# A Mamba selective scan laid out as 4 states x 32 channels on the partitions, with column-strip sums

## What is computed

```
for t in range(L):                      # per batch b, channel d, state n
    h[d, n] = exp(dt[d, t] * A[d, n]) * h[d, n] + dt[d, t] * x[d, t] * Bm[n, t]
    y[d, t] = sum over n of h[d, n] * Cm[n, t]
y = (y + D[d] * x[d, t]) * silu(z)
```

## Time and profile before

| | |
|---|---|
| median of 3 runs | 3600.76 us (3592.4 to 3601.16) |
| the profiled execution | 3599.16 us |
| its span in the profile | 3597.9 us |
| mean granted TensorE clock | 0.966 of full speed |
| busy share over the span | PE 90%, PEld 66%, DVE 61%, ACT 42%, POOL 39% |
| transfers | 273.15 MB, mean 76 GB/s |

### The profile page before, as it was taken

How to read it: one execution, slowest core, us unless ns; L and a number is a source line. 1 busy time by engine, 2 the same in 40 slices (tenths; PEclk the granted TensorE clock), 3 DMA queues, 4 the chain that set the end, 5 groups by cost and what they waited for, 6 DMA issues and landing times. The chain is left out here.

```text
span 3597.9 us, 41339 instructions
## 1 busy us (share of the span) xinstructions
PE 3225.9 (90%) x12763; PEld 2392.0 (66%) x12763; DVE 2197.2 (61%) x1925; ACT 1514.3 (42%) x2148; POOL 1395.1 (39%) x794
## 2 busy tenths in 40 slices
PE   9999677877876689999799999997889999999996
PEld 7877433333332277888577777776668888888884
DVE  6544499999999955711376777774553333333326
ACT  4447644444444332311387778773231121121111
POOL 0002299999999722000377777770100000000001
PEclk9999889999999999999899999998999999999998
DMA  2124521113110075322111111115211111111101
GB/s 110 41 83 160 201 109 61 45 52 143 45 61 30 18 275 198 131 87 93 64 34 34 31 31 35 31 31 195 82 65 47 41 54 47 41 55 52 47 18 58
DMA packets 125427, 273.15 MB, mean 76 GB/s; under 512 B 24448, under 2 KB 38656, under 8 KB 122400
## 3 DMA queue, kind: packets, MB, share of 16 engines
q1 hardware_dynamic: 107632, 262.42, 21.3%
q10 hardware_dynamic: 17712, 9.79, 0.9%
HBM read 207.87 MB, written 64.29 MB: 76 GB/s over the span
## 5 line engine op out<-in xcount | busy, mean ns | idle before, releaser
L799 PE MATMUL scan_ps_y<-scan_g,scan_ident 128*128 128x512 f32 x1024 | 514.3, 635 | 192.1 <-DVE scan_g L730 175.0
L771 POOL TENSOR_TENSOR scan_dbx<-scan_u,scan_b_bc 128x1024 f32<-128x1024 f32 x256 | 594.2, 2354 | 31.9 <-DMA scan_b_bc<-bc 31.9
L1549 POOL TENSOR_TENSOR at_p_lo<-at_p,at_p_hi 128x512 fp32r<-128x512 f32 x384 | 513.3, 1344 | 175.9 <-ACT at_p_hi L1457 163.7
L702 ACT ACTIVATE scan_ps_a<-scan_dt,scan_a_neg 128x512 f32<-128x512 f32 x512 | 328.0, 679 | 442.9 <-DVE scan_g L730 435.8
L799 PEld LDWEIGHTS scan_ps_y<-scan_g,scan_ident 128*128 128x128 f32 x1024 | 191.8, 198 | 481.9 <-DVE scan_g L730 297.5
L927 POOL TENSOR_TENSOR ff_y<-ff_y,ff_rstd 128x512 f32<-128x512 f32 x14 | 24.9, 1806 | 1126.7 <-DVE ff_rstd L916 1126.7
L743 DVE TENSOR_TENSOR_SCAN scan_ps_a<-scan_ps_a,scan_dbx 128x512 f32<-128x512 f32 x384 | 441.6, 1211 | 1.5 <-POOL scan_dbx L771 1.5
L1495 DVE TENSOR_REDUCE at_neg_max<-at_ps_mx 128x1 fp32r<-128x1536 f32 x132 | 231.9, 1757 | 173.6 <-PE at_ps_mx L1569 162.4
L1454 ACT ACTIVATE at_p<-at_ps_s 128x512 f32<-128x512 f32 x384 | 228.1, 594 | 117.5 <-PE at_ps_s L1586 96.3
L1969 DVE TENSOR_TENSOR ff_hf<-ff_sg,ff_ps_u 128x1024 f32<-128x1024 f32 x28 | 34.2, 1221 | 388.6 <-PE ff_ps_u L97 388.6
L1457 ACT ACTIVATE at_p_hi<-at_p 128x512 fp32r<-128x512 f32 x384 | 242.8, 632 | 12.3
(11 more groups left out here) (253 smaller groups left out, 7215.0 us busy)
## 6 DMA issues: line engine op xcount, KB each, us to landing
ff_w<-in_w SPq DMA_DIRECT2D x56, 512.0 KB, 4.2
in_w<-in_w_in SPq DMA_DIRECT2D x32, 512.0 KB, 3.6
mid_w<-in_w_out SPq DMA_DIRECT2D x32, 512.0 KB, 5.3
ff_w<-in_w SPq DMA_DIRECT2D x56, 256.0 KB, 2.6
ff_wo_wo<-in_w_o SPq DMA_DIRECT2D x32, 384.0 KB, 3.1
scan_cx<-in_ctx SPq DMA_DIRECT2D x9, 1024.0 KB, 5.7
sz<-in_xz SPq DMA_DIRECT2D x16, 512.0 KB, 3.1
dt<-in_acc SPq DMA_DIRECT2D x16, 512.0 KB, 3.6
```

Of the source, the lines that this page charges most:

```text
L702: nc.scalar.activation(ps_a[(2 * s + k) % SB][:, h], dt[s][:], ACT.Exp, scale=a_neg[:, it, 2 * k + h:2 * k + h + 1]).then_inc(a_ready, 1)
L771: nc.gpsimd.tensor_tensor(dbx[k % SL][:], u[s][:].unsqueeze(1).to_broadcast([P, 2, L]), b_bc[:, 2 * k:2 * k + 2], ALU.mult).then_inc(dbx_r ...
L799: last = nc.tensor.matmul(ps_y[:], ident[:], g[(2 * s + k) % SB][:, h], start=False, stop=k == NK - 1 and h == 1)
L1549: nc.gpsimd.tensor_tensor(p_lo[t % NSL][:], p[t % NSL][:], f32(p_hi[t % NSL][:]), ALU.subtract).then_inc(p_lo_done, 1)
```

## The change

A block is still 128 channels of one batch, but the partitions now hold 4 groups of states x 32 channels: partition 32a + d is channel d of a strip, and its states are the four of group a. The 128 channels are CG = 4 strips c of CW = 32, which lie along the free dimension. So:

- dt and u are loaded four times, once for each group of partitions, as [128, 4, 512] (`load_spread`: 4 transfers of 256 KB for each tile, where there was one). Two slots each, where there were three.
- The rows of Bm and Cm are loaded with 4 rows to each group of 32 partitions (`load_rows`), for both batches before the loop; nothing is loaded at the change of batch.
- A pair k is now two strips (c = 2(k % 2) and the next) of the state k // 2 of each group. It is still 1024 elements on 128 partitions, and there are still 8 pairs a block.
- DVE scans the pair in one instruction of 1024 elements. A zero decay at element 512, written once before the loop (ACT's second exponential writes elements 513 to 1023), makes the second strip start anew.
- All scans write `g` in SBUF, and all products with Cm are made in place in `g`; 4 slots of `g`, 2 of `ps_a`. A decay slot is free after its scan, where it was free after the product for six pairs of eight.
- PE sums with a [128, 32] selector `sel` (4 identities stacked): each 512 elements are added into a strip of 32 partitions of `ps_y`, so that a matmul sums 4 states. It has 16 such matmuls a block and 4 for the diagonal, where there were 16 and 1. It waits for the products of two pairs (one state of each group) before its 4 matmuls, and DVE waits at every even pair for the sums of the pairs 3 and 4 before.
- xc comes to a tile `xs` by a transfer of 256 KB a block. The 24 key matmuls of a chunk are spread, two after each sum, over the first 12 of the 16 sums of four blocks.

The core of the diff (the rest is names, slots and the blocks' order):

```diff
-    b_bc = sb("b_bc", [P, NS, L])
-    c_bc = sb("c_bc", [P, NS, L])
+    b_bc = sb("b_bc", [P, B, NB, L])
+    c_bc = sb("c_bc", [P, B, NB, L])
+            def load_spread(tile, src, done):
+                for a in range(CG):
+                    sp.dma_start(tile[a * CW:(a + 1) * CW], src.rearrange("(c d) l -> d c l", c=CG)).then_inc(done, 16)
+            def load_rows(tile, b, row, done):
+                for a in range(CG):
+                    r = row + NB * a
+                    sp.dma_start(tile[a * CW:(a + 1) * CW, b], d["bc"][b, r:r + NB].partition_broadcast(CW)).then_inc(done, 16)
...
             def times_c(n, s, k):
-                dve.wait_ge(scanned, 2 * SL + 2 * n + 2)
-                dve.wait_ge(summed, n + 2)
-                nc.vector.tensor_tensor(g[s][:], ps_a[s][:], c_bc[:, 2 * k:2 * k + 2], ALU.mult).then_inc(g_ready, 1)
+            def times_c(n, it, k, b):
+                dve.wait_ge(scanned, SL + n + 1)
+                v = g[k % SG][:].rearrange("p (h l) -> p h l", h=2)
+                nc.vector.tensor_tensor(v, v, c_bc[:, b, k // 2].unsqueeze(1).to_broadcast([P, 2, L]),
+                                        ALU.mult).then_inc(g_ready, 1)
...
-                    for h in range(2):
-                        dve.wait_ge(a_ready, 2 * n + h + 1)
-                        nc.vector.tensor_tensor_scan(out[:, h], ps_a[slot][:, h], dbx[k % SL][:, h], 0.0,
-                                                     ALU.mult, ALU.add).then_inc(scanned, 1)
+                    if k % 2 == 0:
+                        dve.wait_ge(summed, SUM0 + 2 * (n - SG) + CG)
+                    dve.wait_ge(dbx_ready, n + 1)
+                    dve.wait_ge(a_ready, 2 * n + 2)
+                    nc.vector.tensor_tensor_scan(g[k % SG][:], ps_a[k % SA][:], dbx[k % SL][:], 0.0,
+                                                 ALU.mult, ALU.add).then_inc(scanned, 1)
...
-                nc.tensor.matmul(ps_y[:], d_diag[s][:], xc[:, it], start=True, stop=False)
-                for k in range(NK):
-                    wait_product(pe, it, k)
-                    for h in range(2):
-                        last = nc.tensor.matmul(ps_y[:], ident[:], g[(2 * s + k) % SB][:, h], start=False,
-                                                stop=k == NK - 1 and h == 1)
-                    last.then_inc(summed, 1)
+                for c in range(CG):
+                    q = slice(c * CW, (c + 1) * CW)
+                    nc.tensor.matmul(ps_y[q], d_diag[s % 2][:, q], xs[s % 2][:], start=True, stop=False)
+                for m in range(NB):
+                    wait_product(pe, it, 2 * m)
+                    wait_product(pe, it, 2 * m + 1)
+                    for c in range(CG):
+                        h = c % 2
+                        nc.tensor.matmul(ps_y[c * CW:(c + 1) * CW], sel[:], g[(2 * m + c // 2) % SG][:, h * L:(h + 1) * L],
+                                         start=False, stop=m == NB - 1).then_inc(summed, 1)
```

More of the change, by code:

```diff
@@ L560, in blocks, with chunk, is_first @@
     def blocks(eng, body):
[L562 to L569, removed]
+        def chunk(j, b):
+            for s in range(CB):
+                body(CB * j + s, j, s, b)
+        for b in range(B):
+            chunk(PER_B * b, b)
+            with eng.Fori(PER_B * b + 1, PER_B * (b + 1)) as j:
+                chunk(j, b)
+    def is_first(it):
+        return isinstance(it, int) and it == 0
     with nc.Block() as block:
@@ L607, in next_chunk @@
[L607 to L630 removed]
+            def load_chunk(c):
+                sp.dma_start(cx[:], d["ctx"][c // 2][:, :, bass.ds((c % 2) * TOKS, TOKS)]).then_inc(cx_ld, 16)
@@ L658, in _ @@
-            for s in range(SB):
-                sp.wait_ge(y_st[s], 16 * len(range(s, NIT, SB)))
-            sp.wait_ge(k_st, 16 * NU)
-            sp.wait_ge(cx_ld, 16 * (NKC + 1))
+            load_rows(b_bc, 1, 0, b_ld[1])
+            load_rows(c_bc, 1, NS, c_ld[1])
+            for s in range(CB):
+                body(s, 0, s)
+            with sp.Fori(1, NCH - 1) as j:
+                for s in range(CB):
+                    body(CB * j + s, j, s)
+            for s in range(CB):
+                body(NIT - CB + s, NCH - 1, s, last=True)
@@ L663, in _ @@
+            store(NIT - 1, (NIT - 1) % 2)
+            for s in range(2):
+                sp.wait_ge(y_st[s], 16 * NIT // 2)
+            sp.wait_ge(k_st, 16 * KF * NCH)
         @block.scalar
@@ L701, in body @@
                     for h in range(2):
[L702 removed]
+                        c = 2 * (k % 2) + h
+                        nc.scalar.activation(ps_a[k % SA][:, h * L + h:(h + 1) * L], dt[s % 2][:, c, h:L], ACT.Exp,
                                              scale=a_neg[:, it, 2 * k + h:2 * k + h + 1]).then_inc(a_ready, 1)
[L704 to L706 removed]
@@ new lines, in body @@
+                    if (k - 1) % NK in BY_POOL or (is_first(it) and k == 0):
+                        continue
+                    before = isinstance(it, int) and k == 0
+                    if isinstance(it, int) and it % IT == 0 and k == 2:
+                        dve.wait_ge(c_ld[b], 16 * CG)
+                    times_c(n - 1, it, (k - 1) % NK, (it - 1) // IT if before else b)
+            for s in range(SA):
+                nc.vector.memset(ps_a[s][:, L:L + 1], 0.0).then_inc(zeroed, 1)
```

266 lines of the change are left out of this document (110 added, 156 removed).

## The result

The changed kernel takes 3732.96 us (median of 4 runs, 3727.75 to 3740.05) against 3598.16 us for the kernel before (median of 4, one more than in the table ahead): a ratio of 1.0379 with a 95% interval of 1.036 to 1.0398. It is slower by 134.8 us. The forecast was 3745 us, in a range of 3716 to 3785. The profiled execution took 3727.75 us, with a span of 3726.5, and a mean granted clock of 0.876 where it was 0.966.

What follows compares the result with a forecast made beforehand. Turns between POOL's instructions and DVE's products bound the scan: 32 x 29.6 = 947, plus 4, is 951 us against 807, +144 us; 3599.16 becomes 3743, and 1.6 for the median gives 3745 us, range 3716 to 3785.

Steps and rivals of the forecast that it cites:

- The mechanism: In the scan, POOL's SBUF instructions and DVE's two-SBUF-input products can't overlap; their turns set the pace, 29.6 us a block.
- The sum by whole lengths: Upper bound of a block's turns, waits at full instruction lengths: 10 x 2.35 + 6 x 1.22 = 30.8 us.
- The start: Start and end of the scan stage: more bytes before the first dbx against fewer first-block stalls, 0 us within -6 to +6.
- Some 4 us: At the scan's start: time to load 1.5 MB more before the first dbx, at 300 to 430 GB/s.
- the 951 us of the forecast: Scan stage after the change: 32 x 29.6 = 947 us of blocks, and 4 us outside the turns.
- the fill: At the scan stage's ends: 4 us for the first dbx and the last scan and product outside the turns.
- Scans, ACT, transfers: In the scan stage: a 1024-element scan takes 2.28 us; ACT's work and transfers of 2.5 MB a block stay hidden.
- Rival 2: In the scan: DVE's products don't take turns with POOL, DVE sets 24.3 us a block, 3576 us in all; chance 0.07.
- rival 3: In the scan: POOL keeps the ports while it has work queued, 34 us a block, 3886 us; chance 0.04.
- Rival 4: At the last block of four: cx lands late, sums and scans wait, +28 us, 3773 us; chance 0.08.
- Rival 1: In PE's sums: strips run in series, 3.44 us a sum, DVE's even scans stall, +16 us, 3761 us; chance 0.17.
- DVE's slack: In each scan block: 5.3 us that DVE has spare, said to hide its waits for sums at even pairs.

Runs made afterwards that it cites:

- Experiment 1: The change, but DVE's scans for its six pairs write to a PSUM tile, so its products have one input in SBUF: 3633.22 us, ratio to before 1.0102.
- experiment 2: The kernel before with every scan writing g in SBUF and DVE's products made in place there, old layout kept: 3739.8 us, ratio 1.0388.
- experiments 5 and 6: The change with none of the products by POOL (8 + 8 turns): 3656.23 us; the change with one a block by POOL (9 + 7): 3689.3 us.
- experiment 3: The change with 128-column, full-width sum matmuls that run one after the other, still 4 slots of g: 3914.8 us, ratio 1.088.
- experiment 4: The change with full-width sums one after the other, 8 slots of g for 4, and no tile xs: 3733.18 us, ratio 1.0381.

## Why the prediction was right

**The mechanism.** "One block now has 10 POOL instructions and 6 DVE products that must take turns" held. Experiment 1 took the second SBUF input away and the wait went; experiment 2 brought it into the old layout and the wait came; experiments 5 and 6 changed the number of turns and the block followed. That giving DVE more work makes the kernel faster is the sharpest of these, since a DVE that set the pace in the change would have made it slower.

**Its size.** The block was put at 29.6 us, the middle of 29.0 and 30.8, and is 29.06. The prices read from the earlier trace rows, 2.26 and 1.10 us behind a wait, were nearly the right ones for all instructions (2.26 and 1.08), and the allowance above them was not needed: 17 us too much. The sum by whole lengths, 30.8 us, is not met: the change has 29.06, and by 2.35 and 1.22 us the versions with 9 + 7 and 8 + 8 instructions would have 29.7 and 28.6, where they have 27.82 and 26.5.

**The start.** It was costed at 0 within -6 to +6, and POOL's first instruction came 7.5 us later (451.56 for 444.01), outside those bounds. The term failed twice. "Some 4 us" for 1.5 MB more was too little, at 300 to 430 GB/s: the transfers ran at 211 GB/s. And the gain set against it was counted already: the 807.1 us of today hold the first block's stalls of 1.50 and 4.16 us, and the 951 us of the forecast hold none, so the difference of the two has them. The forecast's own 4 us should have stood in the sum in full.

**The sum.** Against the forecast, -18 us for the blocks and the fill and +7.5 for the start, two errors that partly cancel: the stage ends 133.4 us later than before (1384.51 for 1251.11), where 144 were forecast. The stages behind it took 4.8 us less in this execution (2342.0 us for 2346.8), less than the runs of one kernel lie apart (3592.4 to 3601.16 before).

**Scans, ACT, transfers.** 2.28 us a scan was right. ACT and the transfers stayed hidden: DMA share rose from 0.19 to 0.44, and no DVE or POOL instruction waited for a transfer after POOL's first.

**Rivals.** Rival 2 (no blocking) and rival 3 (POOL keeps the ports) are refuted by the block's length and by the product that ended 1.08 us behind POOL's. Rival 4 (late cx) shows once, in the first block: PE stands 7.94 us before its first key matmul, which starts at 474.22, when cx, asked for at 453.17 and 21.0 us on its way, lands, and DVE then waits 5.25 us for the sum behind it. It cost nothing: the next three distances between POOL's products are 14.51, 13.70 and 15.39 us, three times 14.53. At the later chunks PE doesn't wait for cx.

Rival 1 (strips in series) didn't come about, but its price was wrong: "I estimate half a microsecond a block, +16 us", where full-width sums cost 182 us. The steps that failed there are the stalls' size and "These stalls mostly fall on DVE's slack". It had 1.35 us at scans 2 and 6 and 0.2 at the two other even scans, 3.1 us a block; experiment 3 has 1.78 and 2.36, 8.3 a block. The 0.2 that became 2.36 is the sum of 5.40 us at a clock partly at half: "At a low clock [...] it would be more" was said and not priced. DVE's own 24.3 us and 8.3 of stalls are 32.6, more than the slack could take; the block was 34.0, and 34.6 in the mean. That the range held is in this part luck: strips in series had a chance of 0.17 and a place inside the range, and experiment 3, which puts the sums in series, lies 130 us above it.

**What was looked for.** POOL's mean over its ten instructions was forecast near 2.9 us and is 2.91 (3.08 for `dbx`, 2.37 for its products); DVE's products were to be "well over 1.22" and are at 1.87.

## What to carry to other kernels

Before moving an operand from PSUM to SBUF, count the inputs that each DVE instruction then has in SBUF, and how busy POOL is: with two SBUF inputs on DVE and POOL reading SBUF, the lengths of both added up here instead of overlapping, and the sum is a bound of its own beside each engine's work. When such a sum of turns sets the pace, moving work from POOL to DVE can be the faster way. Before counting a stall as hidden, add up the ring that it closes (scan, product, sum, free slot) at the low clock as well as the full one, and hold it against the number of slots. And when the profile names what ended a wait, check that the named instruction is the one that was needed. Take a change of many parts apart: here one part was worth 12 us, another cost about 142 (3739.8 for 3597.51), and what that leaves for the rest (layout, fourfold loads, strips) is some 5 us.

## What the runs showed of the hardware that was not expected

**Strips.** Four matmuls of 32 columns (eight records) ran beside each other. PE's timeline of the change has

```profile
805.21 1.93 PE L784 MATMUL scan_ps_y<-scan_g,scan_sel 128*32 128x512 f32 x8 [4.70 <-DVE scan_g L709]
```

at the lower clock (granted 0.50), and that of experiment 1 has

```profile
800.06 1.07 PE L786 MATMUL scan_ps_y<-scan_g,scan_sel 128*32 128x512 f32 x8 [0.22 <-DVE scan_g L710]
```

at the full one (1.00), against 3.70 us for eight records of 128 columns at the full clock in experiment 3: 3.5 times as fast. That they overlap, and are not just shorter, is in their records: the eight of 1.07 us are 0.59 to 0.62 us each, as long as one of full width (0.59). No row of before could show it. The Trainium skill (TensorE: Matmul & The Clock Gate, "Part 3: Packing small matmuls — row/col tiling") gives 2.38 for three strips, and the trace, with one strip more, goes with that.

**The clock.** With strips PE is busy for 463 of the scan's 928 us, where it was for 610 of 805, and the granted clock over the scan falls from 0.95 to 0.60, which is a mixture of 1.2 and 2.4 GHz. It is the strips and not the slower pace: experiment 4, with the same time and full-width sums, has PE busy for 667 of 928 us and a granted clock of 0.89. The key matmuls' records grow from 379 to 645 ns in the mean. It costs this kernel nothing, because PE waits for DVE either way; in experiment 3, where sums stand in the ring, the low clock costs.

**How the wait of one engine for the other is recorded.** It lies inside the waiting instruction's length, on both engines (3.33 for 2.35 us on POOL, 3.36 for 1.19 on DVE), and not in idle time.
